# Row maxima written into the queries' image by ScalarE, in place of the pick matmuls

## The reference, cut to what matters

```python
def _L1_attn_ref(x, wq, bq, wu, bu):
    HEADS = 16; b, s, emb = x.shape; hd = emb // HEADS
    q = jnp.einsum('bse,oe->bso', x, wq) + bq
    qh = q.reshape(HEADS, b, s, hd)
    kh = qh; vh = qh
    scores = jnp.einsum('hbqd,hbkd->hbqk', qh, kh) * (1 / math.sqrt(emb))
    attn = jax.nn.softmax(scores, axis=-1)
    out = jnp.einsum('hbqk,hbkd->hbqd', attn, vh)
    out = out.reshape(b, s, emb)
    return jnp.einsum('bse,oe->bso', out, wu) + bu
```

## Time and profile before

| | us |
|---|---|
| median of three executions | 2499.76 |
| the three | 2499.36, 2499.76, 2514.42 |
| profiled execution | 2515.66 |
| its span | 2513.9 |

### The profile page before, as it was taken

The page is one execution under the profiler, slowest core; times in us unless marked ns, Lnnn a source line. Parts: engine busy times, 40 slices in busy tenths (PEclk is TensorE's granted clock), DMA queues, the critical chain, the costliest instruction groups (busy, mean ns, idle before and its releaser), DMA issues.

```text
span 2513.9 us, 38918 instructions
## 1 busy us (share of the span) xinstructions
PE 2036.8 (81%) x13610; PEld 1594.7 (63%) x13610; DVE 1426.1 (57%) x4130; ACT 1236.0 (49%) x2670; POOL 648.7 (26%) x663
## 2 busy tenths in 40 slices
PE   2766773587878888998899889989998999788884
PEld 1555552476557556875787578757875886665764
DVE  5877536453556675566556565666566356356522
ACT  3766413444446455555555564555455446335431
POOL 3111003333131133124223322332233124013052
PEclk9777885699889899999899999999999999899997
DMA  7100000112211211312132213221322312312121
GB/s 237 43 1 1 1 1 0 31 45 64 56 47 44 65 52 57 85 55 55 52 91 57 65 39 89 62 65 32 92 67 60 88 52 68 89 29 61 41 62 47
DMA packets 228948, 141.29 MB, mean 56 GB/s; under 512 B 116489, under 2 KB 206732, under 8 KB 228754
## 3 DMA queue, kind: packets, MB, share of 16 engines
q1 hardware_dynamic: 174320, 85.60, 13.4%
q0 software_dynamic: 16960, 34.74, 4.6%
q10 hardware_dynamic: 37474, 18.46, 2.6%
HBM read 82.48 MB, written 57.16 MB: 56 GB/s over the span
## 4 chain that ended last, share of the span: by engine, by line
PE 53%; DVE 24%; ACT 12%; issue 6%; DMA 2%; POOL 2%; SPq 1%; ACTq 0%; POOLq 0%; DVEq 0%
PE PS L908 17%; PE PS L876 9%; DVE AR L1085 3%; PE PS L1207 3%; PE PS L1170 3%; PE PS L1188 3%; PE PS L1433 2%; PE PS L1193 2%; ACT AR L1141 2%; DVE small L332 2%; ACT AR L837 2%; ACT AR L362 2%; DVE AR L795 2%; DVE xnT L1269 1%; PE PS L911 1%
## 5 line engine op out<-in xcount | busy, mean ns | idle before, releaser
L908 PE MATMUL PS<-AR,W 128*128 128x256 f32 x2560 | 653.0, 404 | 20.9 <-DVE AR L795 15.0
L795 DVE TENSOR_TENSOR AR<-AR,PS 128x512 f32<-128x512 f32 (+1 forms) x384 | 228.6, 597 | 653.9 <-ACT AR L837 525.8
L908 PEld LDWEIGHTS PS<-AR,W 128*128 128x128 f32 x2560 | 499.8, 204 | 92.1 <-issue 17.0
L837 ACT ACTIVATE AR<-PS 128x512 f32<-128x512 f32 (+1 forms) x384 | 201.1, 525 | 556.5 <-PE PS L908 439.1
L1085 DVE TENSOR_REDUCE AR<-PS 128x2 f32<-128x512 f32 x512 | 337.2, 688 | 160.0 <-PE PS L1170 155.6
L1141 ACT ACTIVATE AR<-PS 128x512 f32<-128x512 f32 x512 | 303.6, 600 | 236.3 <-PE PS L1193 231.9
L876 PE MATMUL PS<-AR,WO 128*128 128x256 f32 (+1 forms) x1536 | 357.7, 383 | 0.0
L876 PEld LDWEIGHTS PS<-AR,WO 128*128 128x128 f32 (+1 forms) x1536 | 295.5, 193 | 42.8
L1170 PE MATMUL PS<-AR 128*128 128x256 bf16 x1024 | 204.8, 287 | 40.4 <-DVE AR L1085 25.9
L743 POOL DMA_INDIRECT AR<-YE,gidx1c x128 | 128.8, 1007 | 379.8 <-issue 231.4
L743 POOL DMA_INDIRECT AR<-YE,gidx x128 | 128.3, 1002 | 350.9 <-ACT AR L1141 310.8
(11 more groups left out here) (359 smaller groups left out, 2771.5 us busy)
## 6 DMA issues: line engine op xcount, KB each, us to landing
AR<-XE SPq DMA_DIRECT2D x128, 128.0 KB, 2.1
YE<-AR ACTq DMA_DIRECT2D x128, 128.0 KB
AR<-QD SPq DMA_DIRECT2D x384, 32.0 KB
QD<-AR SPq DMA_DIRECT2D x8, 768.0 KB, 5.2
AR<-KD SPq DMA_DIRECT2D x64, 96.0 KB
W<-in_L_ffn_w_kernel_dram SPq DMA_DIRECT2D x2, 2560.0 KB, 13.5
OD<-AR SPq DMA_DIRECT2D x128, 36.0 KB
X<-in_L_attn_dense_dram SPq DMA_DIRECT2D x8, 512.0 KB, 4.5
```

What stands on the lines that cost most here:

```text
L795: ins = dve.tensor_tensor(hf[:, cols], gl[i % 2][:, cols], H[:, 2 * (i % 2) + 1, cols], ALU.mult)
L837: ins = act.activation(gl[i % 2][:, cols], H[:, 2 * (i % 2), cols], ACT.Gelu_apprx_tanh)
L908: mm = pe.matmul(H[:, b0, b * CAP:(b + 1) * CAP], w0[:, e, hb * P:(hb + 1) * P], xeT[e % 2], start=True, stop=True)
```

## The change

The negated, split and turned maxima go into the queries' image itself. Rows 64 to 87 of an image were unused: 24 rows, three parts of each of eight key blocks. The keys' image gets in the same rows a mask (`own`), which is one where the row's block is the block of the column, and else zero; so the one product of keys and queries contains the maxima of its own block. ACT writes the mask once into each of the four key images (`own_act`). Since the maxima are computed from the same image with these rows zero, SP loads 24 zero rows with each piece from another part of the keys' image. The pick matmuls, `pick` and `MP` go.

The maxima of the two query halves stand in two 128-column halves of `MS`, and PE turns them by two matmuls instead of one. ACT's copy goes from 32 rows of PSUM to 32 rows of `QA`, 2048 elements per row: each value is repeated for the eight key blocks. The queries are loaded by three DMAs, whose source repeats 8 rows three times, 8 rows twice, and 8 rows once. Scores run up to 16 blocks ahead instead of 14. Splitting, turning and values take place at slots computed from `scored` (turning at 5, 10, 18, 26, 34, 42, 50; values two or three slots later), before at slots 3, 5 and 2 of each piece.

```diff
-            return min(NS, i + PB + 6, PB + 2 * (i + 1))
+            return min(NS, i + 2 * PB, PB + 2 * (i + 1))
+        SPLIT = [slot_of(PB * (c + 2) - 1) for c in range(NPC - 1)]
+        TURN = [i + 2 for i in SPLIT]
+        VALUES = [TURN[0] + 2] + [i + 3 for i in TURN[1:]]
...
-            for lo, hi, a in ((0, 8, 0), (8, 16, 0), (16, 24, 0), (24, 32, 8), (32, 40, 8), (40, 48, 16)):
-                sp.dma_start(QA[c % DEPTH][lo:hi, :], qr[a:a + hi - lo, :]).then_inc(S["a_kq%d" % (c % DEPTH)], 16)
+            for lo, times, part in ((0, 3, 0), (3 * AD, 2, 1), (5 * AD, 1, 2)):
+                rows = qr[part * AD:(part + 1) * AD].rearrange("(o d) t -> o d t", o=1)
+                sp.dma_start(QA[c % DEPTH][lo:lo + times * AD, :], rows.broadcast_to([times, AD, 2 * QUAD])
+                             ).then_inc(S["a_kq%d" % (c % DEPTH)], 16)
+            sp.dma_start(QA[c % DEPTH][SHIFT:SHIFT + 3 * PB, :],
+                         KA[c % DEPTH][ZEROS:ZEROS + 3 * PB].rearrange("p a t -> p (a t)")
+                         ).then_inc(S["a_kq%d" % (c % DEPTH)], 16)
...
-                m, parts = mx[c % 2].rearrange("p a b -> p (a b)"), MS[c % 2]
+                m, left = mx[c % 2], mrest.rearrange("p (a b) -> p a b", a=2)
+                parts = MS[c % 2][:, :, SHIFT:SHIFT + 3 * PB].rearrange("p q (b a) -> p a q b", a=3)
...
+        def own_act(act, k):
+            view = KA[k][SHIFTS].rearrange("p g (x j) -> p g x j", j=4)
+            act.copy(view, own[SHIFTS, :].rearrange("p (g o j) -> p g o j", g=2, o=1).broadcast_to(
+                [32, 2, QUAD // 4, 4])).then_inc(S["a_kone"], 1)
...
             def turned(c):
-                act.wait_ge(S["a_mxT"], NPC * n + c + 1)
-                act.copy(MP[c % 2], turned_maxima(c)).then_inc(S["a_mp"], 1)
+                k = NPC * n + c
+                act.wait_ge(S["a_mxT"], k + 1)
+                act.copy(QA[c % DEPTH][SHIFTS, :].rearrange("p (g b t) -> p g b t", g=AH, b=PB),
+                         turned_maxima(c)[SHIFTS].rearrange("p (g o t) -> p g o t", g=AH, o=1).broadcast_to(
+                             [32, AH, PB, AB])).then_inc(S["a_mp"], 1)
...
-                if li == 5 and c + 1 < NPC:
-                    turned(c + 1)
+                if i in TURN:
+                    turned(TURN.index(i) + 1)
...
-                pe.transpose(turned_maxima(c), MS[c % 2].rearrange("p a b -> p (a b)"),
-                             identb[:, :]).then_inc(S["a_mxT"], 1)
+                for q in range(2):
+                    mm = pe.transpose(turned_maxima(c)[:, q * P:(q + 1) * P], MS[c % 2][:, q, :], identb[:, :])
+                mm.then_inc(S["a_mxT"], 1)
...
-                for h in range(2):
-                    pe.matmul(o[:, h * 256:(h + 1) * 256], keys(c, P, h, b), queries(c, b), start=(h == 0),
-                              stop=False, skip_group_check=True)
                 if b == 0:
                     pe.wait_ge(S["a_mp"], NPC * n + c + 1)
-                for q in range(2):
-                    mm = pe.matmul(o.rearrange("p (h q t) -> p q h t", h=2, q=2)[:, q],
-                                   pick[:, q * PB + b:q * PB + b + 1].broadcast_to([P, P]),
-                                   MP[c % 2].rearrange("p (o t) -> p o t", o=1).broadcast_to([P, 2, P]),
-                                   start=False, stop=True, skip_group_check=True)
+                for h in range(2):
+                    mm = pe.matmul(o[:, h * 256:(h + 1) * 256], keys(c, P, h, b), queries(c, b), start=True, stop=True)
                 mm.then_inc(S["a_slot"], 1)
...
+                    b.put(*((slot, lambda k=k: own_act(act, k)) for k, slot in enumerate((7, 8, 12, 13))))
...
-            ch.step(pool.memset(pick[:, :], 0.0))
+            ch.step(pool.memset(own[:, :], 1.0))
```

More of the change, by code:

```diff
@@ L57 @@
 DEPTH = 4
-MROWS = 3 * 2 * PB
+SHIFT = P // 2
+SHIFTS = slice(SHIFT, SHIFT + 32)
+ZEROS = SHIFT + 32
 A_SCALE = float(D) ** -0.5
@@ L121, in build @@
         identb = sb("identb", [P, P], BF16)
-        pick = sb("pick", [P, 2 * PB], BF16)
         join = sb("join", [P, AD], BF16)
+        own = sb("own", [P, PB], BF16)
         tri = sb("tri", [P, P], BF16)
@@ L210, in build @@
         mrest = ar.take((2 * PB,))
-        MS = [ar.take((P // (2 * PB), 2 * PB), BF16) for _ in range(2)]
-        MP = [ar.take((P,), BF16) for _ in range(2)]
+        MS = [ar.take((2, P), BF16) for _ in range(2)]
         qTf = tmp[:, :, :].rearrange("p a b -> p (a b)")
@@ L1068, in turned_maxima @@
         def turned_maxima(c):
-            return side_bank(c).bitcast(BF16)[:, 0:P]
+            return side_bank(c).bitcast(BF16)
         def attend_dve(dve, n, ch, beside):
@@ L1109, in attend_dve @@
                 done = scored(i)
-                if c + 1 < NPC:
-                    if li == 2:
-                        values(c + 1)
-                    if li == 3:
-                        split(c + 1)
+                if i in SPLIT:
+                    split(SPLIT.index(i) + 1)
+                if i in VALUES:
+                    values(VALUES.index(i) + 1)
+        def own_act(act, k):
+            view = KA[k][SHIFTS].rearrange("p g (x j) -> p g x j", j=4)
+            act.copy(view, own[SHIFTS, :].rearrange("p (g o j) -> p g o j", g=2, o=1).broadcast_to(
+                [32, 2, QUAD // 4, 4])).then_inc(S["a_kone"], 1)
         def attend_act(act, n, beside, stored=None):
@@ L1150, in values @@
             def values(c):
-                pe.wait_ge(S["a_mp"], NPC * n + max(c, 1))
+                pe.wait_ge(S["a_mp"], NPC * n + c + 1)
                 for b in range(PB):
@@ L1159, in scores @@
             def scores(c, b):
+                if b == 0 and c == 0 and n == 0:
+                    pe.wait_ge(S["a_kone"], DEPTH)
                 if b == 0:
-                    pe.wait_ge(S["a_kq%d" % (c % DEPTH)], 16 * 9 * (NPC // DEPTH * n + c // DEPTH + 1))
+                    pe.wait_ge(S["a_kq%d" % (c % DEPTH)], 16 * 7 * (NPC // DEPTH * n + c // DEPTH + 1))
                 if c >= 1:
@@ L1225, in attend_pe @@
                 shifted(i)
-                if c + 1 < NPC:
-                    if li == 2:
-                        if c == 0:
-                            pe.wait_ge(S["m_ysb"], stored)
-                        values(c + 1)
-                    if li == 5:
-                        maxima(c + 1)
+                if i in TURN:
+                    if i == TURN[0]:
+                        pe.wait_ge(S["m_ysb"], stored)
+                    maxima(TURN.index(i) + 1)
+                if i in VALUES:
+                    values(VALUES.index(i) + 1)
                 if li == 5:
@@ L2519, in _ @@
                                        pattern=[[1, P]], channel_multiplier=-1))
+            ch.step(pool.affine_select(out=own[:, :], in_=own[:, :], compare_op=ALU.is_ge, fill=0.0, base=-SHIFT,
+                                       pattern=[[-3, PB]], channel_multiplier=1))
             ch.link(pool.affine_select(out=avg, in_=avg, compare_op=ALU.is_ge, fill=0.0, base=0,
                                        pattern=[[-LSEG, NLT]], channel_multiplier=1))
+            ch.step(pool.affine_select(out=own[:, :], in_=own[:, :], compare_op=ALU.is_ge, fill=0.0, base=SHIFT + 2,
+                                       pattern=[[3, PB]], channel_multiplier=-1))
             ch.step(pool.affine_select(out=avg, in_=avg, compare_op=ALU.is_ge, fill=0.0, base=LSEG - 1,
```

13 lines of the change are left out of this document (5 added, 8 removed).

## The result

The changed kernel takes 2650.35 us (median of four, 2638.21 to 2659.33), the kernel before beside it on the same chip 2499.56 us: a ratio of 1.0591 [1.0538, 1.0644]. That is 5.9% slower, where the prediction had 6 us faster, and 114 us above the upper end of the range. The profiled execution took 2654.46 us, 139 more than that of before, at a mean granted clock of 0.863 (before 0.909).

A forecast was written before the change was run, and what follows sets the result against it. No engine was taken to fill the span; binding varied by attention stage and part. Seventh stage -6, seven others -3, first copies +1, loads +2 gave -6 us: 2499.76 to 2494 us, range 2452 to 2536.

The forecast's parts named there:

- the term for the long copy: ACT's copy in attention: 1.94 us instead of 0.26, 107 us more ACT work over 64 copies, only partly showing.
- the tail: Last 18 us of the fourth attention stage, standing for six others: one long copy falls here; forecast -0.4 us per stage.
- the front: First 39 us of the fourth attention stage: four long copies offset the picks' gain; sum 0, bounds -4.2 and +2.9 us.
- ACT in PE's place: Slower rival: at early slots PE runs out of score banks behind the copy; +36 us net, 2536 us, chance 0.10.
- The clock: Slower rival in attention: three more falls to half clock per stage, 48 us, 2542 us, chance 0.10.
- balanced case: Whole kernel: the summed terms hold, 2494 us, own range 2476 to 2518, chance 0.48.
- The picks: Pick matmuls in attention: 2.3% of the span on the chain of waits, 57.8 us, the most their deletion can return.
- The loads: SP's loads per piece: 0.66 us less issue against 96 KB of zeros; +1 us in each of two stages, +2 us.
- The rival on broadcast loads: Broadcast query loads use few DMA engines; piece 0 some 2 us later, experts' load late; +17 us, 2511 us, chance 0.12.
- The lookahead: Tail of seven attention stages: scores two blocks further ahead cost +1.6 us, DVE's earlier last maximum gives -1.38 us.
- the seventh stage's piece: Eight slots of the seventh attention stage: PE-bound 8.41 us becomes ACT-bound, 7.47 us, about 7.5 as a sign.
- the fourth stage: Attention stage standing for six others, 82 us before: 80 to 83 us expected after the change, as a sign.

The follow-up runs named there:

- e7: Changed kernel with each slot's two score matmuls issued twice and ACT's copy cut to one key block (256 elements per row): 2571.12 us, 1.0272 of the kernel before.
- e6: Changed kernel with each slot's two score matmuls issued twice, long copy kept: 2648.03 us, 1.0570 of the kernel before.
- f4: Changed kernel with ACT's long copy three slots later and the values two later, first piece unchanged: 2540.64 us, 1.0113 of the kernel before.
- f3: The changed kernel timed again, unaltered, as the measure for its set: 2650.02 us, 1.0555 of the kernel before.
- f1: Kernel before with only the pick matmuls left out, so no maxima are subtracted: 2485.31 us, 0.9902 of the kernel before.
- f2: Kernel before without pick matmuls and with each slot's two score matmuls issued twice: 2508.41 us, 0.9987 of the kernel before.
- e9: Kernel before with only the change's loads, three broadcast loads of queries and the zeros' DMA: 2616.37 us, 1.0110 of the kernel before.
- e2: Changed kernel with the queries loaded by six plain DMAs of 8 rows, zeros' DMA kept: 2696.69 us, 1.0431 of the kernel before.
- e3: Changed kernel without the zeros' DMA, scores for the maxima using only the first 64 rows: 2806.03 us, 1.0863 of the kernel before.
- e10: Kernel before with scores running 16 blocks ahead instead of 14, nothing else: 2593.43 us, 1.0041 of the kernel before.
- e8: Kernel before with pick matmuls on 64 of the 128 rows, same number of matmuls and columns: 2566.25 us, 1.0231 of the kernel before.
- e1: Changed kernel with ACT's copy writing only one key block, 256 elements per row instead of 2048: 2635.32 us, 1.0204 of the kernel before.

## Why the prediction was wrong, step by step

**The step that failed is the term for the long copy**: "I let 1.0 of its 1.67 show" in the tail, 0.4 for two of four in the front, and for the seventh stage the slowest engine's sum, 7.47 us. Together these let 7 x (3.3 + 0.8 + 1.0) + 5.5 x (7.47 - 6.76) = 40 us of the copies show. The mechanism that I gave a chance of 0.10, ACT in PE's place at slots 10, 18 and so on, is what happened. It was written as "each of 56 copies puts its 1.67 us on the path", +94. The runs give 75 us of 96 (e7 against e6, same set), and for the place 111 us (f4 against f3). At slot 5, which the rival names too, no outgoing sum stands ahead of the copy: ACT's sums stand at slots 6, 10, 14 and so on. The argument that ACT may "be late by about one slot before PE stands" was right as a number and was not used: one slot is about 1 us, and exponential, sums, copy and exponential come to 3.3 in a row. Dividing a piece's work by engine (7.47 for ACT) assumes that the queue in between is deep enough to even it out; with two banks it is not. f4 came down to 7.79 us by order alone, so the bound can nearly be reached, but only where PE has other work meanwhile.

**The clock** was a rival of its own, with 0.10, priced apart from ACT's. Here they are one case: a stand of 2 us on ACT is followed by half speed, and then PE, not ACT, is late. In the piece above it is 1.29 of 2.85 us. Had I taken the two rivals together, 94 + 48 - 58, the upper case would have been 2584, with the loads 2601; the range ended at 2536. The row that I set against this rival, 1402 to 1404 at clock 1.00, is read rightly, but it is one gap, and too little to price the others by. Even 2601 is still 49 us short. (The own range of the balanced case does not follow from its terms either: 2494 + 20 x 2/3 is 2507, not 2518.)

**The picks** were taken at 57.8 us, the chain's share, as a ceiling. Alone they are worth 25 us (f1). With PE's work put back (f2) the time goes back as well, so the engine was the bound in part, as I said; but what the deletion frees goes into longer waits (95.0 us instead of 59.4) and a lower clock; how much into which, no run separates.

**The loads**, "+2", failed too: alone they cost 1.1%, 28 us (e9). I counted the issues, "0.66 us less", with 0.33 us for each whatever its shape. A broadcast load takes 1.90 / 3 = 0.63 and the zeros 0.81, so a piece takes 3.8 us instead of 3.05. But the issue is not what PE waits for, as e2 issues no faster and waits 15.0 us. It is the landing, which I took at "+1 each, near the lower end because several engines share". The rival on broadcast loads had this right, with 0.12: "Piece 0 lands some 2 us later" is what e2 and e3 show (PE starts 2.6 to 2.9 us after the issue, or 4.2 to 5.6). It happens seven times and not twice; the experts' input, which it called late, is not (PE's wait for AR<-XE is 7.0 us, before 6.5). The Trainium skill, page "DMA: Bandwidth & Descriptors", section "Why a DMA increments its semaphore by 16 and not by 1", sets the number of engines by the slowest dimension of both sides; by that rule three and two engines would serve these loads. The waits of e2 and e3 agree as far as they go, but no run shows which engines carried a load.

**The lookahead**, +1.6 - 1.38 per stage, nearly nothing, is +0.4% alone (e10), 11 us; no run takes its two parts separately.

**Right** was the copy's duration (1.94 against 1.857), and that PE's idle time before the slots would grow by tens of us. Of the marks that I set, the seventh stage's piece (7.5) came out at 10.75 and the fourth stage (80 to 83) at 95, and the rows at clock 0.50 that I named as a mark of being wrong are there.

**The account**, in per cent: picks -1.0, loads +1.1, lookahead +0.4 and a long copy at the old place +1.3, each measured alone in the kernel before, and +4.4 for the early place, measured in the changed one. They add to 6.2, where 5.4 to 5.9 was measured, on different chips, so the agreement is rough. It can be tested once more: f2, loads and lookahead add to 1.4 and leave out little but the early place of a short copy, but e7 measured 2.7. So about 1.3 belong to the place even with a short copy, or the parts do not simply add. Two things stay open. f4 moves the values' turning too, away from the products that follow it in the changed kernel, and no run moves only one of the two; that f4 (1.0113) comes out below the short copy at the early place (1.0204, on another chip) says that the copy's length there is not all of it. And how much of the whole loss is the clock's stays open: e8 and e3 show that a lower clock costs time without longer waits, e6 raises it only by work that takes time itself.

## What to carry to other kernels

A long instruction on an engine that feeds another through two buffers can cost more by its place than by its length (here 111 us for three slots, against 33 us for the same length at the old place): lay out what the receiver can do meanwhile, instruction by instruction, before moving it, and put it where the receiver's own long work begins. Count waits and clock as one case: here a stand of 2 us brought half speed behind it, one of 0.57 us did not. Three merged broadcast loads issued no quicker than the six that they replaced, and landed 2 us later: ask both of a merged load.

## What the runs showed of the hardware that I had not expected

- With the same number of matmuls and columns, but 64 rows instead of 128, the granted clock was lower: 0.653 in attention (e3), where the changed kernel has 0.822, and 0.940 (e8) where the kernel before has 0.965. e8 lost 2.3% of time by it.
- A thousand added matmuls of 128x256 moved the time by 0.3% in e6, with the clock up from 0.814 to 0.923, and by 0.9% in f2. The second is nearly all that the picks cost (1.0%).
- A copy from PSUM took the same time on 32 partitions as on 128 for a row of 256 elements: 362 ns (e1, bf16) and 368 ns (f32).
- The issue of a DMA on SP took 0.33 us for 8x2048, 0.63 for a broadcast of 8x2048 to 24, 16 or 8 rows (mean of three), and 0.81 for 24x2048 from SBUF to SBUF.
